# DeepFM forward pass on one core: TensorE's signals cut to halves of jobs, and GpSimd's gathers let go by VectorE's picks

## What is computed

```python
sp_emb = emb_tables[fidx, sp_input]          # 2048 x 26 x 32
lin_vals = lin_tables[fidx, sp_input, 0]
lin_output = ds_input @ lin_w.T + lin_b + jnp.sum(lin_vals, axis=1, keepdims=True)
s = jnp.sum(sp_emb, axis=1)
bi_pooled = 0.5 * (s * s - jnp.sum(sp_emb * sp_emb, axis=1))
x = jnp.concatenate([bi_pooled, ds_input], axis=1)
h = jax.nn.relu(x @ w1.T + b1)
h = jax.nn.relu(h @ w2.T + b2)
out = jax.nn.sigmoid(h @ fw.T + fb + lin_output)
```

## Time and profile before

| what | us |
|---|---|
| median of three executions | 459.72 (456.66 to 461.1) |
| span of the profiled execution | 459.0 |
| TensorE products busy | 406.9 (89%) |
| VectorE busy | 331.9 (72%) |
| GpSimd busy | 283.8 (62%) |
| ScalarE busy | 258.8 (56%) |
| TensorE weight loads busy | 335.6 (73%) |

### The profile page before, as it was taken

One profiled execution on the slowest core, in us unless ns is written; L12 is line 12 of the kernel. 1 busy time (PEld: TensorE's weight loads), 2 busy tenths in 40 slices (PEclk: granted clock), 3 DMA queues, 4 the chain that ended last, 5 costly groups with the idle time before them and its releaser, 6 DMA issues.

```text
span 459.0 us, 5550 instructions
## 1 busy us (share of the span) xinstructions
PE 406.9 (89%) x1798; PEld 335.6 (73%) x1798; DVE 331.9 (72%) x357; ACT 258.8 (56%) x450; POOL 283.8 (62%) x308
## 2 busy tenths in 40 slices
PE   8998989899987989879989799889799866998967
PEld 5787877688776878768768588668588744757734
DVE  7778597976689576956929759649569967587733
ACT  6899645765457544746355564565556745552133
POOL 6675575575755766657557567557566575556740
PEclk9998999899999989999999899999899995999979
DMA  7632253232522226223352233422253121122210
GB/s 208 180 45 23 24 125 67 22 24 12 169 22 23 25 11 168 23 24 25 49 142 12 21 25 62 131 23 12 23 136 50 12 15 10 10 13 12 14 10 0
DMA packets 17126, 23.03 MB, mean 50 GB/s; under 512 B 6246, under 2 KB 16184, under 8 KB 16187
## 3 DMA queue, kind: packets, MB, share of 16 engines
q0 software_dynamic: 9536, 5.05, 19.9%
q1 hardware_dynamic: 7560, 17.62, 12.2%
HBM read 22.61 MB, written 0.04 MB: 49 GB/s over the span
## 4 chain that ended last, share of the span: by engine, by line
PE 36%; issue 33%; another core or an unknown queue 9%; ACT 9%; DVE 7%; DMA 5%; SPq 0%; DVEq 0%; ACTq 0%
PE cand L892 16%; PE cand L895 16%; DMA stage<-tabs 5%; ACT gates L719 3%; ACT distance L711 2%; DVE gates L461 2%; DVE masked L486 2%; DVE low L473 1%; ACT high L686 1%; PE cand L939 1%; PE cand L949 1%; PE bank_b L939 1%; ACT bank_a L705 1%; DVE picks L546 1%
## 5 line engine op out<-in xcount | busy, mean ns | idle before, releaser
L367 POOL DMA_INDIRECT rows<-table,row_idx x293 | 278.0, 949 | 156.5 <-issue 72.9
L892 PE MATMUL cand<-high,gates 128*128 128x462 f32 x826 | 318.8, 386 | 18.9 <-issue 17.8
L895 PE MATMUL cand<-low,gates 128*128 128x462 f32 x826 | 315.0, 381 | 15.3 <-issue 15.1
L892 PEld LDWEIGHTS cand<-high,gates 128*128 128x128 f32 x826 | 160.2, 194 | 54.2 <-issue 33.7
L895 PEld LDWEIGHTS cand<-low,gates 128*128 128x128 f32 x826 | 160.2, 194 | 37.9 <-issue 19.5
L486 DVE TENSOR_TENSOR masked<-cand,mask 128x924 f32<-128x924 f32 x58 | 64.8, 1117 | 89.9 <-remote 87.9
L494 DVE TENSOR_REDUCE picks<-masked 128x66 f32<-128x924 f32 x56 | 107.2, 1914 | 1.9
L719 ACT ACTIVATE gates<-distance,one 128x512 fp32r<-128x512 bf16 (+1 forms) x128 | 83.8, 703 | 12.1 <-remote 12.1
L711 ACT ACTIVATE distance<-codes,minus_key 128x512 bf16<-128x512 f16 (+1 forms) x119 | 77.7, 703 | 0.1
L699 ACT COPY bank_b<-high 128x462 f32<-128x462 f32 x47 | 25.8, 549 | 85.8 <-issue 51.5
L461 DVE TENSOR_SCALAR gates<-bank_a,key_of 128x512 fp32r<-128x512 f32 (+1 forms) x82 | 56.1, 739 | 0.5 <-PE bank_b L986 0.5
(11 more groups left out here) (112 smaller groups left out, 126.1 us busy)
## 6 DMA issues: line engine op xcount, KB each, us to landing
stage<-tabs SPq DMA_DIRECT2D x7, 1617.0 KB
rows<-table,row_idx POOLq DMA_INDIRECT x293
codes<-codes_dram SPq DMA_DIRECT2D x27, 128.0 KB
stage<-tabs SPq DMA_DIRECT2D x7, 231.0 KB, 2.9
idx_raw<-sparse SPq DMA_DIRECT2D x1, 208.0 KB
w_sb<-w2t SPq DMA_DIRECT2D x1, 128.0 KB
dense_sb<-dense_cols SPq DMA_DIRECT2D x1, 120.0 KB
x_and_y<-dense_rows SPq DMA_DIRECT2D x1, 112.0 KB
```

The source lines that it names most:

```text
L367: pool.indirect_dma_start(out=to, out_offset=None, in_=table[:, :], in_offset=bass.IndirectOffsetOnAxis(ap=row_idx[:, at:at + 1], axis=0), ...
L892: first = nc.tensor.matmul(to, gate, high[f % 2][:, k, :], start=(k == 0), stop=False)
L895: last = nc.tensor.matmul(to, gate, low[f % 2][:, k, :], start=False, stop=(k == CHUNKS - 1))
```

## The change

TensorE raises `gates_used` once in a job, with the job's last product, and `half_tile_begun` is gone. The waits for `gates_used` count jobs and no longer chunks: both makers of gates wait for the whole of job j-3, VectorE once before its chunks of a job. GpSimd waits for `picked` in place of `half_tile_begun`; its table has an entry for each pick, and lets 14 gathers go before the first pick. `begun_until` becomes `picked_until`.

```diff
-    HALVES = (0, 4)
     AHEAD = 400
-    LET_OF = [[30, 30, 30, 440, 40, 40, 40, 340]] + [[135, 101] * TB] * (NJ - 5) + [[175] * 8, [175] * 8, [150] * 8, [280] * 4]
-    LET = [0] + list(itertools.accumulate(itertools.chain.from_iterable(LET_OF)))
-    assert len(LET) == 1 + sum(SIZE) * len(HALVES)
+    LET_OF = [990] + [472] * (2 * (NJ - 5)) + [700] * 4 + [600] * 2 + [1120]
+    LET = list(itertools.accumulate(LET_OF))
+    assert len(LET) == PAIRS - 1
...
-    def begun_until(n):
-        return min(h for h in range(len(LET)) if AHEAD + LET[h] > 100 * n)
+    def picked_until(n):
+        return min(p for p in range(PAIRS - 1) if AHEAD + LET[p] > 100 * n)
...
-                    if begun_until(n) > 0:
-                        pool.wait_ge(half_tile_begun, begun_until(n))
+                    if picked_until(n) > 0:
+                        pool.wait_ge(picked, picked_until(n))
...
+                if j >= 3:
+                    dve.wait_ge(gates_used, j - 2)
                 for k in range(k0, k1):
                     g = j * CHUNKS + k
-                    if g >= SLOTS:
-                        dve.wait_ge(gates_used, g - SLOTS + 1)
...
-                    dve.wait_ge(gates_used, (j + 1) * CHUNKS)
+                    dve.wait_ge(gates_used, j + 1)
...
-                    dve.wait_ge(gates_used, NJ * CHUNKS)
+                    dve.wait_ge(gates_used, NJ)
...
-                        act.wait_ge(gates_used, FIRST_OF[f - 1] * CHUNKS)
+                        act.wait_ge(gates_used, FIRST_OF[f - 1])
...
                 act.wait_ge(distance_made, ACT_UNTIL[j] + k + 1)
-                if g >= SLOTS:
-                    act.wait_ge(gates_used, g - SLOTS + 1)
+                if j >= 3:
+                    act.wait_ge(gates_used, j - 2)
...
-                first = nc.tensor.matmul(to, gate, high[f % 2][:, k, :], start=(k == 0), stop=False)
-                if k in HALVES:
-                    first.then_inc(half_tile_begun, 1)
+                nc.tensor.matmul(to, gate, high[f % 2][:, k, :], start=(k == 0), stop=False)
                 last = nc.tensor.matmul(to, gate, low[f % 2][:, k, :], start=False, stop=(k == CHUNKS - 1))
-                if i == SIZE[j] - 1:
+                if i == SIZE[j] - 1 and k == CHUNKS - 1:
                     last.then_inc(gates_used, 1)
```

More of the change, by code:

```diff
@@ L262, in build_deep_fm @@
         act_gates = sem("act_gates")
-        half_tile_begun = sem("half_tile_begun")
         half_matched = sem("half_matched")
```

## The result

The changed kernel takes 496.86 us (median of five executions, 494.5 to 509.58), beside 459.72 us for the kernel before (five executions, 456.66 to 461.7): a ratio of 1.078, 95% interval 1.0735 to 1.0826. It is 8% slower, where 451.5 us was forecast and 430 to 465 given as the range.

A forecast was written before the change was run, and what follows sets the result against it. The prediction took TensorE to bound the kernel, losing time to stalls with late signals. 459.0 less 8 us for signals, other terms 0, gave 451.0 of span, 451.7 as median; forecast 451.5 us, range 430 to 465.

The forecast's parts named there:

- Cost: 0: GpSimd's gathers: letting them go by picks, about a job ahead, was claimed to cost 0 us.
- What bounds the kernel: TensorE's body, 35 to 365 us: 51 us lost, 9 to half-rate clock and 42 to stalls where TensorE's signals come late.
- Signals of TensorE: Removing 416 of TensorE's signals, at up to 0.03 us each in the stalling stretch, was to save 8 us.
- whether the completion of TensorE's work is what runs short: Unread step behind the signals' saving in the stalling stretch; if false, the 8 us term is nothing.
- Coarser `gates_used`: Waits of VectorE's and ScalarE's gates counted in jobs: cost 0 to 0.7 us, gain at most 0.5, taken as 0.
- Behind a waiting gather only other gathers are queued: GpSimd's queue: a gather that waits delays only further gathers, so cost 0.
- nobody waits for rows: Users of gathered rows: no waiting after the change, with the last gather starting around 434 us.
- the net is earlier or equal nearly everywhere: Release of GpSimd's gathers: picks come some us after the tiles, but about a job ahead, so gathers start no later.
- Slower: Rival: shifted TensorE pauses bring more clock falls, 1.5 us each, 467 us with five more; chance 0.13.
- nothing makes the pauses longer: Reason given against more clock falls: the change does not lengthen TensorE's pauses.
- No gain: Rival: signals ride along with TensorE's products and stalls have another cause, 459.7 us; chance 0.37.
- The stalls go with the signals: Rival: pending signals bring TensorE's stalls, so removing 416 of 514 takes most away, 418 us; chance 0.10.

The follow-up runs named there:

- e2_wait_only: Kernel before with all TensorE signals kept, only GpSimd's wait and its table changed to wait for picks: 503.47 us beside 460.69, ratio 1.0904.
- e4_free_run: Kernel before with GpSimd's gathers not paced, held only by the full ring of row buffers: 613.41 us beside 460.69, single execution.
- e1_gates_only: Kernel before with only the coarser `gates_used`, once a job, 180 signals fewer, `half_tile_begun` kept: 460.18 us beside 460.69, ratio 0.9977.
- a3_after: The changed kernel measured a second time, untouched, beside the kernel before: 495.1 us beside 461.54, ratio 1.0726.
- e3_half_gathers: Kernel before without every second gather of tiles 0 to 14, all waits kept: 393.46 us beside 460.69, ratio 0.854, single execution.
- a4_after: The changed kernel, untouched, in a set without stalls, beside the kernel before: 388.31 us beside 388.39, ratio 0.9997.

## Why the prediction was wrong, point by point

The step that failed is the gathers' "Cost: 0": the wait moved from TensorE's signals to picks costs 42.8 us by itself (e2_wait_only, 503.47 beside 460.69). The gain that was to come from the signals, 8 us, isn't there either.

**What bounds the kernel.** Right as far as it went: the stalls are late signals of TensorE, let go all at once. The prediction went on to say that TensorE's own signals might be what runs short. That was an inference from which thing was late, not from what ended the lateness. The rows had it: in the earlier trace rows GpSimd's wait of 3.04 us began at 202.21, and TensorE flowed again 2.2 us after that. I listed GpSimd there as one of three engines that wait; by e4_free_run it was the one whose waiting ended the stall.

**Signals of TensorE, 8 us.** This is the gain that failed, and with its doubt named ("whether the completion of TensorE's work is what runs short"). It measured next to nothing: 180 signals fewer, -0.5 us (-3 to +0.9); 590 more, 0.3 us without stalls and 3.1 us (2.4 to 5.5) with them. The 0.03 us in the burst of the earlier trace rows is how close together held signals arrive, not what one costs. The per-tile tail of the Trainium skill's page "TensorE: Matmul & The Clock Gate" ("The cost: per-tile semaphore tail") doesn't show in these runs: by its 26 ns the 590 signals would be an estimated 15 us. They aren't raised by concurrent products on tiles of the array, as in the case it tells of.

**Coarser `gates_used`, 0.** Right: e1_gates_only. The changed kernel's longer wait of ScalarE (27.5 us for 12.1) goes with the longer stalls; with e1's waits alone the time didn't move.

**Gathers, "Cost: 0".** This is where the loss is. "Behind a waiting gather only other gathers are queued" and "nobody waits for rows" are true of the changed kernel too (the squares idle 0.1 us), and beside the point: it asked who needs the gathers' rows, and not what the gathers do to others while they run, nor what their pauses were for. The last gather starts at 470.71 and not at 434: the picks that let the gathers go come later themselves, with TensorE's body slower by 6%. The step "the net is earlier or equal nearly everywhere" held only where there are no stalls.

**The rivals.** *Slower* named more falls of the clock behind stalls, 1.5 us each, and gave as reason against it that "nothing makes the pauses longer". That reason was false. Windows at half rate went from six of 3.0 us to eight of 4.5, 9 us in the body, and the longer stalls themselves cost 12 (a3_after beside before). The rival had the right place and missed the loop that kept the pauses short. *No gain* is what e1_gates_only showed for 180 of the signals, and what the whole change does where there are no stalls. *The stalls go with the signals*: they don't; they go with the gathers (e3_half_gathers, 393 us).

**The chances.** 0.13 for slower was too low, and the range too narrow above. The term that moves a wait to another signal was priced only by who waits behind it.

## What to carry to other kernels

Where a wait is moved to another signal, look at what the old one did in the worst moments of the trace: a signal that stops its waiter within a gather when its sender is in trouble is a brake, and one that is let go in portions of five and by way of a third engine is not. In a stall ask which engine went quiet just ahead of its end, and not only who was waiting. And a stall that isn't in the program's own dependences may not be there in the next set of runs: the same two kernels differ by 7 to 8% on one chip and by nothing on another.

## What the runs showed of the hardware that I had not expected

- In three of the five sets, indirect gathers of GpSimd, one every 1.25 us without a break, hold TensorE, mostly from 13 to 15.5 us after the run's start (in one case, the first run of e4_free_run, only from 24.6): products start 0.7 to 2.8 us apart, seldom more, VectorE waits up to 9.1 us for signals of theirs (112.0 us in all in a3_after), and all is let go mostly 2 to 3.5 us after the last gather of a run of 12 to 19 ends, 10.7 us after one of 76. Pauses of about 3 us after every ten gathers keep most of it away (112.0 to 20.1 us of late signals).
- In the other two sets nothing of this is there: an unbroken run of gathers through the whole kernel leaves TensorE at 0.214 us per product, 388 us beside 460 us. The gathers themselves are as quick in both kinds, one in 1.25 us. I found no row that tells the kinds apart ahead of a stall; the packets of the gathers' queue take about the same, 18.8% of 494.0 us in a3_after and 23.0% of 386.0 us in a4_after, 93 and 89 us. What inside the chip holds TensorE's signals stays open; that it's the gathers, and their density, is shown, how isn't.
- Behind a long stall the window at half rate was mostly longer too: in a3_after seven of the eight windows have 11 to 14 products (up to 5.4 us), in the kernel before all six have 6 to 9. In the trace of the first measurement of the changed kernel they have 4 to 15.
